# Four fused stages on one core: the first batch's state-space sum and the weight quantisation are done by other engines, in another order

## The chip, the cores and the metric

One core of a Trainium2 chip. Time is microseconds (us) of the device for one execution of the whole program; the median of three runs counts.

## What is computed

x is 4 batches of 512 rows by 512 columns (fp32), ctx is 4 batches of 512 by 256. Four stages follow one another, each with a residual:

```python
x = x + tanh(g_xattn[0]) * mamba(ctx, layernorm(x))          # hidden from ctx, gate from x
x = x + tanh(g_ffn[0])   * bit_ffn(layernorm(x))             # silu(gate) * val, then out; hidden 2048
x = x + tanh(g_xattn[1]) * cross_attention(layernorm(x), ctx) # 16 heads of 128, keys and values from ctx
x = x + tanh(g_ffn[1])   * experts(layernorm(x))             # 4 experts, row j goes to expert j % 4
# inside mamba, for each of 512 channels and 16 states n, over the 512 positions t:
state = state * exp(delta_t * A) + delta_t * u_t * B_t
y_t   = sum_n state_n * C_t,n  +  D * u_t ;  y = y * silu(z)
# inside bit_ffn every linear layer works on rounded numbers:
x_q = clip(round(x * 127 / max|x|), -128, 127) / scale ;  w_q = clip(round(w / mean|w|), -1, 1) * mean|w|
```

## The kernel before

One program holds six streams of work. M is mamba, F the bit feed-forward with the turn of x for the attention (XT), Q the quantisation of the three feed-forward weights, K the keys and values of all batches, A the attention (64 heads: 16 for each batch, then the output projection every 4 heads), E the experts. Each stream is a list of parts (`MAMBA`, `FFN`, `QUANT`, `KV`, `ATTN`, `EXP`), and each engine has a generator for each stream that issues its instructions of the next part. Which stream an engine serves next is fixed when the program is built: `plan()` places all parts on the engines by costs written in the code (for instance `("DVE", 2.45)` for a scan) and by priorities (`FIRST`), and each engine then issues in that order. So an engine never overtakes: where an instruction waits for a semaphore, all that stands behind it on that engine waits too.

What depends on what: M(0) must end before F(0) starts; F(b) before the attention of batch b; all of K (4 quarters of the heads by 4 batches, 16 groups) before the first head; M(b+1) and F(b+1) run beside the attention of batch b. TensorE (PE) fills its time with K as long as batch 0 is in M and F, and with A afterwards.

Mamba, per batch: convolution of 4 taps (`conv`, ScalarE L1171 copies, DVE L882 and L885), silu (L1175), two projections (`xp`, `dt`: L572, L1178, L581, L1183, L1184), softplus (`exp` L1187, `one` L889 and L1192, `soft` L898 to L906), then `init` (D * u, L911) and the loop over 16 states by 2 halves of the channels, so 32 terms of 128x1024. A term is `mul` (L922: delta*u times B), `scan` (L927), `out` (L932: times C), all on DVE, with both operands in SBUF. ScalarE makes the decays exp(delta*A) two instructions a term (L1164) into two buffers, one term ahead. The term is then added into `u` by a DMA that accumulates, issued by GpSimd:

```python
e.dma_start(u[:, 2 * g:2 * g + 2, :], two(wy[s]), accum_op=ALU.add).then_inc(S[f"d_w{s}"], 16)
```

Three buffers `wy` hold terms; `mul` of term i waits until term i-3 is added. B and C come broadcast from HBM (`s_bc<-bc_scratch`, L1524). After the loop: row statistics of x (`ln`, L824 to L828, and a power on GpSimd, L1367), `hn` (L943, waits for the last three additions), silu (L1202), `gate` (L947), four transposes on PE (`yt`, L589) and the residual (L950).

Quantisation, for the three weights w = 0 to 2 in four pieces c of 128x2048: load into a staging buffer (SP, L1471, L1473), sum of |w| on ScalarE (`abs`, L1146), the total through PE (L545), its inverse on DVE (L843 to L847), two DVE passes (L854: times the inverse, at most 1; L856: at least -1, plus MAGIC, which rounds) and a ScalarE pass to fp8 (`put`, L1151). `bias` does the bias rows (L861 to L869, ScalarE L1154). F(0) waits for all 12 `put`.

Feed-forward, for each tile t of 128 rows: entry `e` (statistics; L976, L978, `quant_row` L954 to L962; 5 transposes L611), 4 parts `m` of two banks (matmuls L600; tanh L1220; DVE L1003, L1011), leave `l`: maximum of |h| over 128x2048 (L1014), `quant_row` on 2048 columns (L960, L962), 16 transposes (L637), copies (L1226), 16 matmuls (L645), residual (L1026). K on PE: L679 (keys), L684 (values), L691 (norms), with ScalarE copies L1246, L1249, L1252. The attention starts with L710.

## Time and profile before

| what | us |
|---|---|
| three runs | 2015.21, 2017.95, 2027.63 (median 2017.95) |
| the profiled execution's own time | 2014.32 |
| its span, first to last instruction | 2012.5 |
| first scan of M(0) starts, last ends | 84.8, 253.0 |
| M(0) has written x | 284.6 |
| F(0) starts to normalise | 307.0 |
| first matmul of the attention | 472.2 |

The page gives busy time by engine. A busy share is an average over stages with different limits, so the stages are read one by one: the rows below give, for stretches of the span, the busy time of each engine and the granted clock of TensorE as a share of 2.4 GHz (0.5 is the level 1.2 GHz). The timeline gives start and duration of single instructions, with the idle time of the engine before them and what ended it.

### The profile page before, as it was taken

Reading aid. Unit: us, or ns where it says so; the run is one execution under the profiler, and the core shown is the slowest. Engines: PE = TensorE matmul, PEld = TensorE weight load, DVE = VectorE, ACT = ScalarE, POOL = GpSimd, SP = SyncE. Lnnn points to the kernel's source line nnn. Section 1 sums busy time; section 2 is a strip of 40 time slices with the busy share of each in tenths; the row PEclk is TensorE's granted clock in tenths of the full one; section 3 lists DMA queues with packets and bytes.
Section 4 is the critical chain, followed back from the end, with each engine's and each line's share of the span. In section 5 each row is a group of like instructions: output and inputs, shape, how many; then the busy total and the mean of one; then the engine's idle time right before and its main releaser. Section 6 shows DMA issues by size and latency. Waiting matters only on the chain.

```text
span 2012.5 us, 20103 instructions
## 1 busy us (share of the span) xinstructions
PE 1856.5 (92%) x6442; PEld 884.7 (44%) x6442; DVE 1386.6 (69%) x2076; ACT 936.6 (47%) x1848; POOL 616.6 (31%) x621
## 2 busy tenths in 40 slices
PE   7799998977998799999978999999998989999999
PEld 3355453433444234544433454444444434444543
DVE  4789876899996869988865999896764354431321
ACT  5856565544754355654624555654433333330100
POOL 1133321123644114454610335554312342320100
PEclk8789988988999889999988999999999999999999
DMA  6699952176775003887810257884101399874210
GB/s 236 210 265 284 275 181 101 53 202 154 195 194 140 12 22 94 206 207 186 205 56 18 58 152 180 243 199 117 43 21 59 112 277 272 254 208 183 94 52 32
DMA packets 159463, 304.40 MB, mean 151 GB/s; under 512 B 13944, under 2 KB 46968, under 8 KB 156416
## 3 DMA queue, kind: packets, MB, share of 16 engines
q1 hardware_dynamic: 140928, 236.01, 37.5%
q0 software_dynamic: 18432, 67.12, 17.2%
...
HBM read 177.64 MB, written 58.33 MB: 117 GB/s over the span
## 4 chain that ended last, share of the span: by engine, by line
PE 72%; DVE 11%; ACT 5%; issue 4%; DMA 4%; POOL 2%; SPq 1%; DVEq 0%; ACTq 0%; POOLq 0%
PE p L757 9%; PE p L710 8%; PE p L747 8%; PE p L727 8%; PE p L684 6%; PE p L794 6%; PE p L679 4%; PE p L600 4%; PE p L733 4%; PE p L691 3%; PE p L809 3%; PE p L645 2%; DMA s_U<-in_Wq 2%; PE p L581 1%; DVE s_U L1057 1%
## 5 line engine op out<-in xcount | busy, mean ns | idle before, releaser
L927 DVE TENSOR_TENSOR_SCAN s_M<-s_M 128x1024 f32<-128x1024 f32 x128 | 302.9, 2367 | 18.2 <-ACT s_M L1164 15.7
L1057 DVE CUSTOM_DVE_ANT_0 s_U<-p,s_U 128x512 f32<-128x512 f32 x256 | 187.3, 744 | 171.5 <-PE p L727 169.1
L727 PE MATMUL p<-s_U 128*128 128x512 f32 x512 | 269.3, 613 | 1.8 <-DMA s_U<-k_scratch 1.2
L710 PE MATMUL p<-s_U 128*128 128x512 f32 x512 | 254.7, 604 | 12.7 <-DMA s_U<-in_Wq 11.0
L1383 POOL DMA_DIRECT2D s_u<-s_M x128 | 113.5, 887 | 436.4 <-DVE s_M L932 395.7
L1427 POOL TENSOR_SCALAR s_U<-s_U 128x512 f32<-128x512 f32 x256 | 227.7, 913 | 5.9
L757 PE MATMUL p<-s_U 128*128 128x512 f32 x512 | 223.6, 592 | 0.0
L747 PE MATMUL p<-s_U 128*128 128x512 f32 x472 | 212.9, 594 | 2.4 <-DMA s_U<-p_scratch 1.6
L1294 ACT ACTIVATE s_U<-s_U 128x512 f32<-128x512 f32 x256 | 181.8, 719 | 57.4 <-DVE s_U L1061 57.4
L1299 ACT COPY s_U<-p 128x512 f32<-128x512 f32 x196 | 107.0, 591 | 173.8 <-PE p L733 170.3
L1164 ACT ACTIVATE s_M<-s_dl,s_small 128x511 f32<-128x511 f32 x256 | 170.3, 717 | 33.0 <-DVE s_M L927 32.8
L1423 POOL TENSOR_TENSOR s_U<-s_U,s_mone 128x4 f32<-128x4 f32 x64 | 79.5, 1242 | 294.6 <-ACT s_U L1294 294.4
L922 DVE TENSOR_TENSOR s_M<-s_du,s_bc 128x1024 f32<-128x1024 f32 x128 | 157.1, 1227 | 12.9 <-DMA s_bc<-bc_scratch 8.7
L932 DVE TENSOR_TENSOR s_M<-s_M,s_bc 128x1024 f32<-128x1024 f32 x128 | 156.3, 1221 | 2.3
L757 PEld LDWEIGHTS p<-s_U 128*128 128x128 f32 x512 | 96.8, 190 | 119.0 <-issue 118.6
L710 PEld LDWEIGHTS p<-s_U 128*128 128x128 f32 x512 | 95.0, 195 | 111.3 <-issue 95.2
L684 PE MATMUL p<-s_U 128*128 128x512 f32 x256 | 136.3, 675 | 5.9 <-ACT s_U L1249 2.6
L747 PEld LDWEIGHTS p<-s_U 128*128 128x128 f32 x472 | 89.6, 191 | 116.6 <-issue 114.1
L600 PE MATMUL p<-s_wq,s_U 128*128 128x512 fp8e4 x512 | 136.3, 414 | 0.0
L1367 POOL TENSOR_TENSOR s_U<-s_U,s_mhalf 128x4 f32<-128x4 f32 (+1 forms) x80 | 96.0, 1200 | 128.4 <-ACT s_U L1288 105.5
L679 PE MATMUL p<-s_U 128*128 128x512 f32 x256 | 116.1, 601 | 16.1 <-ACT s_U L1252 14.5
L727 PEld LDWEIGHTS p<-s_U 128*128 128x128 f32 x512 | 88.3, 193 | 81.8 <-issue 78.6
(178 smaller groups left out, 2509.4 us busy)
## 6 DMA issues: line engine op xcount, KB each, us to landing
s_u<-s_M POOLq DMA_DIRECT2D x128, 512.0 KB, 7.3
s_bc<-bc_scratch SPq DMA_DIRECT2D x128, 256.0 KB, 4.9
...
```

The lines of the kernel that those rows point to most:

```text
L600: ins = e.matmul(banks[bk][:], xT[t % 2][:, k, :], wt[:, k, ch * 512:(ch + 1) * 512], start=False, stop=(k == 3))
L679: ins = e.matmul(banks[bk][:], wk[:, k, i * 128:(i + 1) * 128], cT[b][:, k, :], start=(k == 0), stop=(k == 1))
L684: ins = e.matmul(banks[bk][:], cT[b][:, k, i * 128:(i + 1) * 128], wv[:, k, :], start=(k == 0), stop=(k == 1))
L710: ins = e.matmul(banks[bk][:], wqq[j % 2][:, k, :], axT[b % 2][:, k, :], start=(k == 0), stop=(k == 3))
L727: e.matmul(banks[bk][:], qT[j % 3][:, k * 128:(k + 1) * 128], kT[j % 2], start=True, stop=True).then_inc(S["a_s"], 1)
L747: ins = e.matmul(banks[bk][:], V[v][:, kt, :], now[:, kt], start=(kt == 0), stop=(kt == 3))
L757: ins = e.matmul(banks[bk][:], OT[h][:, k * 128:(k + 1) * 128], wo[h], start=(i == 0), stop=(i == GH - 1))
L927: e.tensor_tensor_scan(w, dA[i % 2], w, 0.0, ALU.mult, ALU.add).then_inc(S["m_s"], 1)
L1057: e.tensor_tensor_reduce(out=Pm[j % 2][:, k, :], in0=banks[ABANK[kind, j, k]][:], in1=rkb[j % 2], scale=rq[:, k:k + 1], scalar=-3.0e38, op ...
L1164: e.activation(av[:, t, 1:512], dl[:, 2 * g + t, 1:512], ACT.Exp, scale=Aneg[:, 2 * g + t, n:n + 1]).then_inc(S["m_da"], 1)
L1294: e.activation(Pm[j % 2][:, k, :], Pm[j % 2][:, k, :], ACT.Exp, bias=nm[:, k:k + 1], scale=1.0, accum_out=sm[:, k:k + 1]).then_inc(S["a_e" ...
L1427: e.tensor_scalar(P, P, rc[:, k - 1:k], 1.0, ALU.mult, ALU.mult).then_inc(S["a_pd"], 1)
```

## The change

It has four parts.

1. In batch 0, GpSimd adds each term into `u` itself (a tensor_tensor add of 128x1024, both operands in SBUF) in place of the accumulating DMA. Batches 1 to 3 keep the DMA. D * u moves behind the first scan, the zero columns of the decay buffers are set inside `soft`, and `init` (the first decays) moves between the two halves of `soft`.
2. Quantisation: `thr` (total and inverse), then for each piece `rnd` on ScalarE (scale, plus MAGIC, in place), `clip` on DVE (between MAGIC-1 and MAGIC+1), `put` on ScalarE. The staging loads of w = 1 and 2 are issued by ScalarE behind the `put` that frees the buffer.
3. The planner gets these parts with costs, later loads for the first pieces (17, 4, 9 and 5 in place of 5 each), and the priority on DVE is AFQMKE in place of AFMQKE. Its GpSimd cost for an addition is 2.6. So the order changes on every engine.
4. Feed-forward, all batches: the maximum of |h| is taken in four pieces, one behind each `m`, and a small one over the four; the last pass of `quant_row` on h is cut in two so that the first 8 transposes wait for half; the 5th transpose of the entry waits for its padding alone. Some semaphores are merged; the scores' matmul now waits for `a_qs` (the square behind the copy) in place of `a_qc`.

```diff
-    QUANT += [("abs", w, c) for c in range(4)] + [("put", w, c) for c in range(4)]
+    QUANT += [("abs", w, c) for c in range(4)] + [("thr", w, 0)]
+    for c in range(5):
+        QUANT += [("rnd", w, c)] if c < 4 else []
+        QUANT += [("put", w, c - 1)] if c else []
+        QUANT += [("clip", w, c)] if c < 4 else []
...
-MAMBA += [("soft", i) for i in range(8)] + [("init", 0)]
+MAMBA += [("soft", i) for i in range(4)] + [("init", 0)] + [("soft", i) for i in range(4, 8)]
...
-            part((kind, i), [("DVE", 1.3), ("POOL", 0.8), ("SUM", 5.0)])
+            part((kind, i), [("DVE", 1.3)] + ([("POOL", 0.8), ("SUM", 5.0)] if b else [("POOL", 2.6)]))
...
-FIRST = {"PE": "MFAQKE", "DVE": "AFMQKE", "ACT": "AFMQKE", "POOL": "MAFQKE", "DMA": "QMAFKE", "SUM": "MAFQKE"}
+FIRST = {"PE": "MFAQKE", "DVE": "AFQMKE", "ACT": "AFMQKE", "POOL": "MAFQKE", "DMA": "QMAFKE", "SUM": "MAFQKE"}
...
-                        e.tensor_scalar(src, src, thr[:, w:w + 1], 1.0, ALU.mult, ALU.min).then_inc(*v.up())
-                        e.wait_ge(*v.now())
-                        e.tensor_scalar(src, src, -1.0, MAGIC, ALU.max, ALU.add).then_inc(S["q_rnd"], 1)
+                    elif kind == "clip":
+                        e.wait_ge(S["q_rnd"], 4 * w + c + 1)
+                        e.tensor_scalar(stg[c], stg[c], MAGIC - 1.0, MAGIC + 1.0, ALU.max, ALU.min).then_inc(S["q_cut"], 1)
...
+                    elif kind == "rnd":
+                        e.activation(stg[c], stg[c], ACT.Copy, bias=MAGIC, scale=thr[:, w:w + 1]).then_inc(S["q_rnd"], 1)
...
+                        if w < 2:
+                            e.wait_ge(S["q_put"], i + 1)
+                            load_stage(e, w + 1, c)
...
-                        e.dma_start(u[:, 2 * g:2 * g + 2, :], two(wy[s]), accum_op=ALU.add).then_inc(S[f"d_w{s}"], 16)
+                            e.wait_ge(*added(b, i - 2))
+                        y = u[:, 2 * g:2 * g + 2, :]
+                        if b:
+                            e.dma_start(y, two(wy[s]), accum_op=ALU.add).then_inc(S[f"d_w{s}"], 16)
+                        else:
+                            e.tensor_tensor(y, y, two(wy[s]), ALU.add).then_inc(S["m_ad"], 1)
...
-                        e.wait_ge(S["f_hq"], 4 * b + t + 1)
+                        e.wait_ge(S["f_hq"], 2 * (4 * b + t) + k)
...
+                        e.tensor_reduce(qt[:, 24 + ch:25 + ch], h[:, ch * 512:(ch + 1) * 512], AXX, ALU.max, apply_absolute_value=True).then_inc(*v.up())
...
-                        e.tensor_reduce(qt[:, 16:17], h, AXX, ALU.max, apply_absolute_value=True).then_inc(*v.up())
+                        e.tensor_reduce(qt[:, 16:17], qt[:, 24:28], AXX, ALU.max).then_inc(*v.up())
```

How the order moves, at three places. First GpSimd, from its first norm of K on: `s_krs` are the norms of K, `s_u` the sum of mamba, `s_M` a term. Before:

```order
L1367 TENSOR_TENSOR s_krs<-s_krs,s_mhalf 128x16
L1383 DMA s_u<-s_M 128x1024
L1367 TENSOR_TENSOR s_krs<-s_krs,s_mhalf 128x16
L1383 DMA s_u<-s_M 128x1024 x3
L1367 TENSOR_TENSOR s_krs<-s_krs,s_mhalf 128x16
```

And now:

```order
L1397 TENSOR_TENSOR s_krs<-s_krs,s_mhalf 128x16
L1416 TENSOR_TENSOR s_u<-s_u,s_M 128x1024 x2
L1397 TENSOR_TENSOR s_krs<-s_krs,s_mhalf 128x16
L1416 TENSOR_TENSOR s_u<-s_u,s_M 128x1024 x6
L1397 TENSOR_TENSOR s_krs<-s_krs,s_mhalf 128x16
```

The 32 DMA issues of batch 0 have become 32 adds, with the norms of K strewn between them: fewer norms for as many terms than before.

Second DVE, from the last passes of `soft` to the second scan (L927 before, L941 now, where `s_M` is written from `s_M` alone; in the row before it both name `s_du`). `s_wab`, `s_gam`, `s_thr` and 128x2048 are quantisation. Before:

```order
L906 TENSOR_TENSOR s_du<-s_dl,s_u 128x1024
L843 TENSOR_REDUCE s_wab<-s_wab 128x1
L845 TENSOR_SCALAR s_gam<-p 128x1
L847 RECIPROCAL s_thr<-s_gam 128x1
L852 TENSOR_SCALAR s_U<-s_U,s_thr 128x512
L854 TENSOR_SCALAR s_U<-s_U,s_thr 128x2048
L856 TENSOR_SCALAR s_U<-s_U 128x2048
L911 TENSOR_SCALAR s_u<-s_u,s_small 128x512 x4
L913 MEMSET s_M 128x2 x2
L922 TENSOR_TENSOR s_M<-s_du,s_bc 128x1024
L854 TENSOR_SCALAR s_U<-s_U,s_thr 128x2048
L856 TENSOR_SCALAR s_U<-s_U 128x2048
```

And now:

```order
L923 TENSOR_TENSOR s_dl<-s_dl,s_M 128x1024
L877 TENSOR_SCALAR s_U<-s_U 128x2048
L925 TENSOR_TENSOR s_dl<-s_dl,s_du 128x1024
L877 TENSOR_SCALAR s_U<-s_U 128x2048
L927 TENSOR_TENSOR s_du<-s_dl,s_u 128x1024
L929 MEMSET s_M 128x2
L936 TENSOR_TENSOR s_M<-s_du,s_bc 128x1024
L877 TENSOR_SCALAR s_x<-s_x 128x2048
L941 SCALAR_TENSOR_TENSOR s_M<-s_M 128x1024
L945 TENSOR_SCALAR s_u<-s_u,s_small 128x512 x4
L877 TENSOR_SCALAR s_U<-s_U 128x2048
L950 TENSOR_TENSOR s_M<-s_M,s_bc 128x1024
```

In the old order weight 0 is quantised ahead of these rows and weight 1 at them; now it is weight 0 here, with three `clip` ahead of the first scan and one behind it. The eight `clip` of weights 1 and 2 and the five bias passes stand among later terms of M(0); before, the last two pieces of weight 1, the bias and weight 2 stood behind its last term.

Third PE, around the transposes of M(0) (L589 before, L610 now). Before:

```order
L679 MATMUL p<-s_U 128x512 x8
L684 MATMUL p<-s_U 128x512 x2
L589 MATMUL p<-s_identf,s_M 128x128 x8
L684 MATMUL p<-s_U 128x512 x2
L691 MATMUL p<-s_ones,s_U 128x1 x16
L589 MATMUL p<-s_identf,s_M 128x128 x8
```

And now:

```order
L702 MATMUL p<-s_U 128x512 x8
L707 MATMUL p<-s_U 128x512 x4
L610 MATMUL p<-s_identf,s_M 128x128 x8
L714 MATMUL p<-s_ones,s_U 128x1 x16
L610 MATMUL p<-s_identf,s_M 128x128 x8
L707 MATMUL p<-s_U 128x512 x2
```

The neighbourhood is alike, the place is not: before, 96 of the 128 key matmuls stand ahead of the first transpose, so 12 of the 16 groups of K; now 80, so 10. On ScalarE the four `abs` of weight 0, which stood among the convolution's copies and around silu, now stand behind silu (two of them) and around `exp`.

## Rows read from the trace of the kernel before

**Rows 1.** The page: span, and busy time by engine.
```profile
span 2012.5 us, 20103 instructions
PE 1856.5 (92%) x6442; PEld 884.7 (44%) x6442; DVE 1386.6 (69%) x2076; ACT 936.6 (47%) x1848; POOL 616.6 (31%) x621
```

**Rows 2.** Windows by stage: us; PE, PEld, DVE, ACT, POOL busy; clock, DMA share, GB/s.
```profile
73.00:254.00 181.00, 178.81 (x620) 98.45 (x619) 156.60 (x109) 108.11 (x196) 63.40 (x40) 0.93 0.99 272
...
285.00:307.00 22.00, 19.92 (x46) 8.70 (x45) 16.61 (x22) 15.14 (x21) 4.58 (x3) 0.95 0.24 85
307.00:472.00 165.00, 141.31 (x578) 69.34 (x576) 132.45 (x205) 73.99 (x124) 30.05 (x24) 0.86 0.43 124
...
654.00:804.00 150.00, 130.59 (x520) 55.53 (x519) 122.05 (x230) 67.52 (x122) 35.88 (x34) 0.89 0.18 43
```

**Rows 3.** DVE by line, 84 to 254 us: busy us, mean ns, idle before, releasers.
```profile
L927 DVE TENSOR_TENSOR_SCAN s_M<-s_M 128x1024 f32<-128x1024 f32 x32 | 73.3, 2292 | 15.2 <-ACT s_M L1164 14.5
L932 DVE TENSOR_TENSOR s_M<-s_M,s_bc 128x1024 f32<-128x1024 f32 x32 | 39.2, 1225 | 1.1
L922 DVE TENSOR_TENSOR s_M<-s_du,s_bc 128x1024 f32<-128x1024 f32 x31 | 37.8, 1220 | 4.7 <-DMA s_u<-s_M 3.9 <-DMA s_bc<-bc_scratch 0.5
L856 DVE TENSOR_SCALAR s_U<-s_U 128x2048 f32<-128x2048 f32 x1 | 1.2, 1226 | 0.0
```

**Rows 4.** Timeline of POOL and DVE where they meet: start us, us, instruction.
```profile
763.17 0.70 POOL L1427 TENSOR_SCALAR s_U<-s_U 128x512 f32<-128x512 f32 x1
...
763.28 1.66 DVE L922 TENSOR_TENSOR s_M<-s_du,s_bc 128x1024 f32<-128x1024 f32 x1
...
763.85 1.66 POOL L1427 TENSOR_SCALAR s_U<-s_U 128x512 f32<-128x512 f32 x1
...
591.35 2.61 DVE L927 TENSOR_TENSOR_SCAN s_M<-s_M 128x1024 f32<-128x1024 f32 x1
...
591.80 2.66 POOL L1427 TENSOR_SCALAR s_U<-s_U 128x512 f32<-128x512 f32 x1
```

**Rows 5.** POOL by line, whole span.
```profile
L1383 POOL DMA_DIRECT2D s_u<-s_M x128 | 113.5, 887 | 436.4 <-DVE s_M L932 395.7 <-DMA s_u<-s_M 31.1 <-issue 9.7
...
L1399 POOL TENSOR_TENSOR s_x<-s_x,s_obt 128x512 f32<-128x512 f32 x16 | 20.3, 1268 | 62.9 <-DVE s_U L976 62.9
```

**Rows 6.** Timeline of ACT and DVE up to the first scan.
```profile
29.10 1.91 ACT L1146 ACTIVATE s_U<-s_x 128x2048 bf16<-128x2048 f32 x1 [4.15 <-DMA s_x<-in_gateT]
...
62.23 1.23 DVE L898 SCALAR_TENSOR_TENSOR s_M<-s_M 128x1024 f32<-128x1024 f32 x1 [3.28 <-ACT s_dl L1192]
...
76.25 0.16 DVE L845 TENSOR_SCALAR s_gam<-p 128x1 f32<-128x1 f32 x1 [3.89 <-PE p L545]
...
84.76 2.29 DVE L927 TENSOR_TENSOR_SCAN s_M<-s_M 128x1024 f32<-128x1024 f32 x1
```

**Rows 7.** Timeline of DVE from the last term of M(0) to F(0).
```profile
253.00 1.22 DVE L932 TENSOR_TENSOR s_M<-s_M,s_bc 128x1024 f32<-128x1024 f32 x1
...
258.17 1.28 DVE L854 TENSOR_SCALAR s_x<-s_x,s_thr 128x2048 f32<-128x2048 f32 x1
...
283.00 1.60 DVE L950 SCALAR_TENSOR_TENSOR s_x<-p,s_gts,s_x 128x512 f32<-128x512 f32 x2 [5.21 <-PE p L589]
...
307.04 0.55 DVE L976 TENSOR_SCALAR s_U<-s_x,s_fq 128x512 f32<-128x512 f32 x1 [0.74 <-POOL s_fq L1367]
```

**Rows 8.** The chain: norms of two successive groups of K, and the attention's start.
```profile
159.21 3.47 PE p L691 x32
...
176.52 3.46 PE p L691 x32
...
472.19 3.69 PE p L710 x8
```

**Rows 9.** DVE by line, whole span: leaving a tile of the feed-forward.
```profile
L1014 DVE TENSOR_REDUCE s_fq<-s_U 128x1 f32<-128x2048 f32 x16 | 36.5, 2278 | 0.2
...
L962 DVE TENSOR_SCALAR s_U<-s_U 128x2048 bf16<-128x2048 f32 x16 | 20.4, 1274 | 0.6
```

More of the change, by code:

```diff
@@ L229, in forward @@
             if k % 2:
-                part(name, [("DVE", 1.6)], ("m", t, k - 1), free=pair)
+                part(name, [("DVE", 2.3)], ("m", t, k - 1), free=pair)
             else:
@@ L242, in forward @@
         elif k == 0:
-            part(name, [("DVE", 5.4)], ("m", t, 7))
+            part(name, [("DVE", 3.6)], ("m", t, 7))
         elif k < 3:
@@ L540, in pe_quant @@
                 for kind, w, c in QUANT:
-                    if kind == "put" and c == 0:
+                    if kind == "thr":
                         e.wait_ge(S["p_set"], 8)
@@ L839, in dve_quant @@
                 for kind, w, c in QUANT:
-                    if kind == "put":
-                        if c == 0:
+                    if kind == "thr":
                             e.wait_ge(S["q_abs"], 4 * w + 4)
@@ L927, in dve_mamba @@
                         e.tensor_tensor_scan(w, dA[i % 2], w, 0.0, ALU.mult, ALU.add).then_inc(S["m_s"], 1)
+                        if i == 0:
+                            e.wait_ge(S["m_h0"], 2 * b + 2)
+                            for t in range(4):
+                                e.tensor_scalar(u[:, t, :], u[:, t, :], Dv[:, t:t + 1], None, ALU.mult).then_inc(*v.up())
                     elif kind == "out":
                         n, g = divmod(i, 2)
-                        w = two(wy[term(b, i)[0]])
+                        w = two(wy[term(b, i)])
                         e.wait_ge(S["m_s"], 32 * b + i + 1)
@@ L951, in dve_mamba, with quant_row @@
                     yield
-            def quant_row(src, amax, dst, sc, mul, last):
+            def quant_row(src, amax, dst, sc, mul, done):
                 e.tensor_scalar(sc[:, 0:1], amax, mul, EPS, ALU.mult, ALU.max).then_inc(*v.up())
@@ L961, in quant_row @@
                 e.wait_ge(*v.now())
-                e.tensor_scalar(dst, src, MAGIC, 127.0, ALU.subtract, ALU.min).then_inc(*(last or v.up()))
+                n = src.shape[1] // len(done)
+                for i, up in enumerate(done):
+                    e.tensor_scalar(dst[:, n * i:n * i + n], src[:, n * i:n * i + n], MAGIC, 127.0, ALU.subtract, ALU.min).then_inc(*up)
             def dve_ffn(b):
@@ L1508, in sp_quant @@
                 for kind, w, c in QUANT:
-                    if kind == "abs" and (w or c >= 2):
-                        load_stage(w, c)
+                    if kind == "abs" and w == 0 and c >= 2:
+                        load_stage(e, w, c)
                     if (kind, w, c) == QUANT[-1]:
```

117 lines of the change are left out of this document (59 added, 58 removed).

## The prediction

> **What bounds the kernel now.** I read the page first: TensorE is busy 92% of the span [rows 1], so time can only come from its idle time, its clock, or the order of the start. Then the windows by stage [rows 2]. From 73 to 254 us PE is busy 178.8 of 181 us, all with K, while DVE runs M(0)'s loop. From 307 to 472 PE is busy 141.3 of 165 us: 23.7 us idle, at a mean clock of 0.86. A feed-forward stretch beside attention (654 to 804) has 19.4 us idle; the two later ones have 18 and 9. In the attention between them PE is nearly full. So the chain is M(0), F(0), the attention's start at 472.2 us [rows 8], and from there 1540 us in which PE sets the pace. What delays the attention's start is paid at the end nearly in full, because PE can do no A before it and has only K to fill with.
>
> M(0)'s loop is DVE's [rows 3]: 73.3 + 39.2 + 37.8 = 150.3 us of scans and products between 84.8 and 254.2 us, thus 4.7 us a term, and about 19 us idle, 14.5 of it waiting for ScalarE's decays. The accumulating DMAs cost DVE only 3.9 us there. So the DMA that is replaced is hardly on the path.
>
> **GpSimd's adds, the term that decides.** The trace has no GpSimd instruction of 128x1024, but it shows what one does to DVE [rows 4]. Alone, L1427 takes 0.70 us. At 763.17 it starts; DVE's product L922 starts at 763.28 and takes 1.66 us where it takes 1.22 [rows 3]: it stood until L1427 ended at 763.87. The next L1427, started at 763.85, took 1.66 us: it stood until the product had read, and ended 0.56 us behind it. A scan fares alike: 2.61 us in place of 2.29 with L1427 ahead of it, and the L1427 behind took 2.66. They take turns, and neither runs beside the other. All three DVE instructions of a term are of this kind, each with both inputs in SBUF. In the old batch 0 GpSimd only issued DMAs there, 0.89 us each [rows 5], and the products kept their 1.22 us.
>
> The Trainium skill ("SBUF — State Buffer", section "Who interferes with whom") says that a DVE instruction with two SBUF inputs and a GpSimd instruction that reads SBUF exclude each other for the whole instruction, also when DVE is in no fast mode. The rows agree with it, for GpSimd instructions with one input; by the rule the whole add would be exclusive as well, which gives the sum below, and a hold shorter than the add gives the second rival.
>
> The add's own length: 128x512 with two inputs takes 1.268 us [rows 5]. For 128x1024 I take 2.4 us (twice that less some fixed part; bounds 1.27 and 2.54). The same skill ("GPSIMD Engine Reference", section 3.1 "Elementwise — side-by-side cycle accounting") lists 4497 ns for 2048 elements, so an estimate of 2.25 us by that page; the sum would be 5 us lower.
>
> Cost on DVE: 32 x 2.4 = 77 us. Bounds: 0 if the adds fall beside DVE, 32 x 2.54 = 81 us.
>
> **Up to the first scan.** Before, ScalarE's copies and silu stand behind `abs`, one of which waited 4.15 us for its load until 29.1 [rows 6]. Now silu can start at about 24 in place of 31.1, and of the four quantisation passes of 1.91 us between silu and Ln two remain in the way: L898 starts at about 52 in place of 62.2. From there to the first scan were 22.5 us; now I take 20: 9.8 for `soft`, 3.7 for three clips, 1.2 for the product, 1 for the inverse, 4 for PE's total as at 76.25 [rows 6]. First scan at 72: 13 us early (bounds 5 and 18, by how far ScalarE's rounding passes hold up the clips).
>
> **The loop.** The same 150.3 us; nine clips of 1.23 [rows 3] make 11.1; five bias passes, four of them like a 1.22 us product, 5.4; D * u and two inverses 3.1: together 170. Two waits for PE's total, 4 each: 8. The 77 us of adds. The old wait for decays goes: ScalarE gets 77 us more time, which also covers most of its 24 rounding and writing passes. Sum 255; the last term ends at 72 + 255 = 327, where it was 254.2 [rows 7]: 73 us late.
>
> **From there to F(0).** Before: 30.4 us until x was written at 284.6, with four passes of two pieces (5 us), the bias and 5.2 us for PE's transposes in between [rows 7]; then 22.4 us until 307.04, which were weight 2. Now all this lies in the loop. I take 22 us (statistics 4, `hn` 1.9, silu and gate 4, transposes with a norm group between them 10, residual 2) and 2.5 us. F(0) starts at 327 + 24.5 = 351.5: 44.5 us late.
>
> **F(0) beside the rest of K.** Before the transposes of M(0), PE has 10 groups of K in its queue and not 12. A group is 17.3 us (176.52 - 159.21 [rows 8]); ten of them are done long before 345, so PE stands still for some 100 us and may not go on, and the two groups, 34.6 us, come behind it. Of the 23.7 us idle there [rows 2] I let half be filled by them, and the finer waits give 3: 34.6 - 12 - 3 = +20 us. The attention starts at 472 + 44.5 + 20 = 536.5.
>
> **The finer waits.** Per tile the maximum of 2.28 us becomes a small one of 0.15 behind a piece of about 0.7, and half of the 1.27 us pass comes off the first transposes [rows 9]: 1.4 + 0.6 = 2.0 us a tile from the chain. For the 12 tiles of batches 1 to 3 that is 24 us at most, and attention covers part of it: I take 10 (bounds 0 and 24). DVE has 0.6 us more per tile. The scores' wait for the square costs nothing, since the square stands a head earlier.
>
> **Sum.** 2014.3 + 44.5 + 20 - 10 = 2069 us, against the profiled execution's own time of 2014.3. The median of the runs is 3.6 us above that, which is less than I can resolve; I leave it out.
>
> **Rivals.**
> First, the same, but nothing is won back: K's two groups come in full (+34.6), the finer waits give nothing, and M(0) is 10 us later still because clips wait for ScalarE. 2014.3 + 44.5 + 34.6 + 10 = 2103. For it: every engine issues in a fixed order that was planned without the blocking. Against it: idle time of 23.7 us is there to fill.
> Second, half a price: the add holds DVE up only for about 1.27 us. The loop loses 36 us less: 2069 - 36 = 2033. For it: no row has an add beside a product. Against it: L1427 blocks for its whole length.
> Third, the adds lie beside DVE. Then the loop is 178 us, but ScalarE's extra passes (24 of 1.91 us beside decays and K's copies, at 108 of 181 us busy [rows 2]) keep the 15 us wait for decays: 193, last term at 265, F(0) at 289.5, 17.5 us early; K's groups +20, waits -10: 2007. Rows 4 speak against it.
> Fourth, on the other side: nothing blocks, the decays come in time too, K fills all 23.7 us, and the finer waits give all they can. F(0) at 274.5 (-32.5), +34.6 - 23.7 - 8 = +3, -24: 2014 - 53 = 1961. Its mechanism is F(0) starting early, because the quantisation no longer stands between M(0) and F(0); it decides from the point where the scans keep 2.29 us beside the adds. For it: those 22 us are really there [rows 2, 7]. Against it: the loop is DVE's, and rows 4.
>
> **Chances.** The forecast 0.48 (its own range 2048 to 2090), first rival 0.17, second 0.14, third 0.13, fourth 0.08. A measurement of this kernel tells about 1% from no change, so 2038 and more is slower. The second case lies across that bound. Slower: 0.48 + 0.17 + 0.10 = 0.75; within 1%: 0.04 + 0.13 = 0.17; faster: 0.08. The range: below 2022 lie the last two cases without their upper tail, above 2102 part of the first, together about 0.2. So 2022 to 2102.
>
> **What the new profile would show.** GpSimd's adds of 2.4 us or more in the records (their wait counted in), scans and products of batch 0 with means well above 2.29 and 1.22 us, unlike those of batches 1 to 3; terms 7.2 us or more apart; the first scan near 72 and F(0) near 350; PE idle by some 100 us ahead of the transposes, with a lower granted clock there; the attention's start near 536. I am wrong if the scans of batch 0 stay at 2.29 us; if the terms lie under 6 us apart; or if PE goes on with K all through M(0).

## The result, and the profile after

The changed kernel takes 2071.02 us (median of 4 runs, 2064.48 to 2075.08), the kernel before 2016.68 (4 runs): a ratio of 1.0254, 95% interval 1.0205 to 1.0303, thus slower, by some 50 us. The prediction was 2069. The profiled execution of the changed kernel has a span of 2073.2 us, 60.7 more than the 2012.5 of the one before; it is the longest of its four and the one before a short one, so stages compared by these two show some 6 to 10 us more than the medians and the ratio do.

The page of the changed kernel:

```profile
span 2073.2 us, 20183 instructions
...
PE 1869.4 (90%) x6442; PEld 883.7 (43%) x6442; DVE 1438.7 (69%) x2144; ACT 959.2 (46%) x1860; POOL 695.5 (34%) x621
...
PE   8546889999699689998977999989999989999999
...
PEclk8767988899799889999988999999999999999999
...
L1416 POOL TENSOR_TENSOR s_u<-s_u,s_M 128x1024 f32<-128x1024 f32 x32 | 109.1, 3409 | 122.0 <-DVE s_M L950 122.0
...
```

PE is busy 90% of the span where it was 92% [rows 1]. The low digits of PE and of its clock stand in the first six slices, the first 310 us: the time was lost at the start. The windows by stage say how much (columns as in [rows 2]):

```profile
76.00:305.00 229.00, 154.22 (x462) 79.88 (x463) 223.86 (x121) 139.09 (x197) 139.58 (x38) 0.78 0.44 141
...
327.00:526.00 199.00, 190.22 (x742) 94.74 (x741) 159.96 (x247) 98.71 (x171) 45.87 (x31) 0.91 0.47 130
...
0.00:526.00 526.00, 424.35 (x1433) 214.49 (x1434) 425.30 (x434) 295.50 (x445) 198.90 (x90) 0.84 0.47 145
526.00:2073.00 1547.00, 1445.08 (x5009) 669.23 (x5009) 1013.40 (x1711) 663.74 (x1415) 496.62 (x532) 0.97 0.50 137
...
```

The last two lines split the span at the first matmul of the attention. Up to there PE stands still for 526.0 - 424.4 = 101.7 us; before it were 472.2 - 412.4 = 59.8 us. So the attention starts 53.8 us late, of which 41.9 us are idle time. The other 12.0 us are PE busy for longer with the same work, and they go with a lower granted clock (0.78 in M(0)'s loop, where PE stops and starts; 0.93 in that stage before [rows 2]). Behind the attention's start the two differ by 1547.0 - 1539.8 = 7 us. M(0)'s loop alone holds 74.8 us of PE's idle time, where it held 2.2 [rows 2].

The milestones that the prediction spoke of, from the timeline of DVE and PE:

```profile
...
76.22 2.28 DVE L941 TENSOR_TENSOR_SCAN s_M<-s_M 128x1024 f32<-128x1024 f32 x1
...
304.77 1.23 DVE L950 TENSOR_TENSOR s_M<-s_M,s_bc 128x1024 f32<-128x1024 f32 x1
...
326.49 0.55 DVE L995 TENSOR_SCALAR s_U<-s_x,s_fq 128x512 f32<-128x512 f32 x1 [0.73 <-POOL s_fq L1397]
...
526.01 2.04 PE L733 MATMUL p<-s_U 128*128 128x512 f32 x2 [4.46 <-DMA s_U<-in_Wq]
```

First scan at 76.2 (84.8 [rows 6]), last term done at 306.0 (254.2 [rows 7]), F(0) normalises at 326.5 (307.0 [rows 7]), attention at 526.0 (472.2 [rows 8]). So F(0) starts 19.5 us late, and from F(0) to the attention another 34 us are lost, though PE is idle there for 8.8 us only (327 to 526), 4.5 of them for the load of Wq in the last row. It does K that was left over. By line, PE's products with the keys' weights (16 to a group of K) in that stretch, before (307 to 472) and now (two fences):

```profile
L679 PE MATMUL p<-s_U 128*128 128x512 f32 x48 | 22.0, 594 | 1.6 <-ACT s_krs L1257 1.6
```

```profile
L702 PE MATMUL p<-s_U 128*128 128x512 f32 x96 | 44.0, 601 | 0.3 <-ACT s_krs L1287 0.3
```

So six groups were left at F(0)'s start, and before only three.

DVE in M(0)'s loop, by form; and, in the second fence, one term in the timeline of DVE and GpSimd, with the last add behind it:

```profile
L941 DVE TENSOR_TENSOR_SCAN s_M<-s_M 128x1024 f32<-128x1024 f32 x32 | 112.3, 3508 | 2.5 <-ACT s_M L1195 1.6
L950 DVE TENSOR_TENSOR s_M<-s_M,s_bc 128x1024 f32<-128x1024 f32 x32 | 50.9, 1591 | 0.8
...
L877 DVE TENSOR_SCALAR s_U<-s_U 128x2048 f32<-128x2048 f32 x7 | 10.6, 1514 | 0.0
...
```

```profile
231.87 1.22 DVE L936 TENSOR_TENSOR s_M<-s_du,s_bc 128x1024 f32<-128x1024 f32 x1
233.12 4.32 DVE L941 TENSOR_TENSOR_SCAN s_M<-s_M 128x1024 f32<-128x1024 f32 x1
...
237.47 1.22 DVE L950 TENSOR_TENSOR s_M<-s_M,s_bc 128x1024 f32<-128x1024 f32 x1
238.61 1.22 DVE L936 TENSOR_TENSOR s_M<-s_du,s_bc 128x1024 f32<-128x1024 f32 x1
239.86 2.29 DVE L941 TENSOR_TENSOR_SCAN s_M<-s_M 128x1024 f32<-128x1024 f32 x1
...
232.03 3.26 POOL L1416 TENSOR_TENSOR s_u<-s_u,s_M 128x1024 f32<-128x1024 f32 x1 [3.48 <-DVE s_M L950]
235.25 4.89 POOL L1397 TENSOR_TENSOR s_krs<-s_krs,s_mhalf 128x16 f32<-128x16 f32 x1
...
306.07 2.35 POOL L1416 TENSOR_TENSOR s_u<-s_u,s_M 128x1024 f32<-128x1024 f32 x1 [3.48 <-DVE s_M L950]
...
310.61 3.20 POOL L1397 TENSOR_TENSOR s_krs<-s_krs,s_mhalf 128x16 f32<-128x16 f32 x1
...
305.91 0.69 DVE L847 BATCH_NORM_STATS2 s_st<-s_x 128x6 f32<-128x512 f32 x1
...
310.04 1.91 DVE L960 TENSOR_SCALAR s_M<-s_x,s_st 128x512 f32<-128x512 f32 x4
...
```

The scan is read with the GpSimd row beside it. The add is issued at 232.03, behind the end of `out`. DVE's `mul` has started at 231.87 and keeps its 1.22 us; the add stands until it is over, at 233.09, and runs then. The scan, issued at 233.12, takes 4.32 us in place of 2.29 [rows 3]: it stood for 2.03 us. The scan at 239.86 has no add in front and takes 2.29; the add's place there is taken by the power on 128x16, issued at 235.25, which takes 4.89 us between DVE's instructions, 3.20 at 310.61, where DVE first runs passes of one input (L960), and 2.93 in e1 below, where DVE is idle beside it. It does not hold DVE as the adds do: while it runs, DVE's `out`, `mul` and scan keep 1.22, 1.22 and 2.29 us. A term is 6.74 us (238.61 - 231.87) and was 4.7. The last add has no DVE instruction with two SBUF inputs beside it: it takes 2.35 us, and DVE's statistics beside it keep their 0.69. Summed over the loop, against the means before [rows 3]: scans +39, `out` +12, `mul` +4, the clips L877 +2, and +2 on one bias pass (L885, 3.19 us here, 1.28 in e1 below): 59 us.

What PE waited for before F(0) (columns: us in total, times, longest), and the timeline of PE and ScalarE in the longest of these stops:

```profile
PE p L702 <- ACT s_krs L1287: 45.1, 4, 20.2
...
```

```profile
...
137.03 3.78 PE L702 MATMUL p<-s_U 128*128 128x512 f32 x4 [20.17 <-ACT s_krs L1287]
...
106.40 0.57 ACT L1282 COPY s_U<-p 128x512 f32<-128x512 f32 x1
111.75 3.90 ACT L1172 ACTIVATE s_U<-s_U,s_thr 128x2048 f32<-128x2048 f32 x2 [4.78 <-DVE s_thr L869]
...
116.77 1.90 ACT L1177 ACTIVATE s_wq<-s_U 128x2048 fp8e4<-128x2048 f32 x1
...
119.14 2.00 ACT L1172 ACTIVATE s_x<-s_x,s_thr 128x2048 f32<-128x2048 f32 x1 [0.47 <-ACT s_wq L1177]
...
133.01 1.91 ACT L1177 ACTIVATE s_wq<-s_U 128x2048 fp8e4<-128x2048 f32 x1 [2.80 <-DVE s_U L877]
...
136.32 0.58 ACT L1282 COPY s_U<-p 128x512 f32<-128x512 f32 x1
136.79 0.19 ACT L1287 ACTIVATE s_krs<-p 128x16 f32<-128x16 f32 x1
...
```

PE does not stand for want of K. It has K in its queue, and waits for K's banks: from 116.9 to 137.0 for L1287, the norms' copy. ScalarE took a K copy at 106.40 and the next at 136.32; in between stand the four rounding passes of weight 1 (L1172, two of them in one row), its four writing passes (L1177), three pairs of decays and a bias cast (not all shown), with a wait of 4.8 us for the inverse of weight 1's total (L869) and one of 2.8 us for a clip (L877). ScalarE issues in its fixed order, so the copies that would free PE's banks wait behind the quantisation.

### The profile page after: what moved, and what is told of

Same layout as the page of the kernel before. It is cut to its first block, busy times and chain, and to the rows that moved or that the text cites. A ratio compares the mean times of both kernels' runs of the same rounds, so it can differ in the third digit from the quotient of the medians.

```text
span 2073.2 us, 20183 instructions
## 1 busy us (share of the span) xinstructions
PE 1869.4 (90%) x6442; PEld 883.7 (43%) x6442; DVE 1438.7 (69%) x2144; ACT 959.2 (46%) x1860; POOL 695.5 (34%) x621
## 4 chain that ended last, share of the span: by engine, by line
PE 62%; DVE 12%; issue 8%; ACT 6%; DMA 5%; POOL 5%; SPq 1%; ACTq 0%; DVEq 0%; POOLq 0%
PE p L780 7%; PE p L733 7%; PE p L770 7%; PE p L750 7%; PE p L621 5%; PE p L817 5%; DVE s_M L941 5%; PE p L702 4%; PE p L707 3%; PE p L832 3%; PE p L756 3%; PE p L668 2%; DMA s_u<-s_M 2%; POOL s_U L1460 2%; DMA s_U<-in_Wq 2%
## 5 line engine op out<-in xcount | busy, mean ns | idle before, releaser
L941 DVE TENSOR_TENSOR_SCAN s_M<-s_M 128x1024 f32<-128x1024 f32 x128 | 341.6, 2669 | 15.8 <-ACT s_M L1195 12.9
L750 PE MATMUL p<-s_U 128*128 128x512 f32 x512 | 271.7, 619 | 12.7 <-DMA s_U<-k_scratch 8.3
L733 PE MATMUL p<-s_U 128*128 128x512 f32 x512 | 257.8, 611 | 14.9 <-DMA s_U<-in_Wq 14.6
L780 PE MATMUL p<-s_U 128*128 128x512 f32 x512 | 223.8, 593 | 0.0
L770 PE MATMUL p<-s_U 128*128 128x512 f32 x472 | 212.6, 593 | 3.2 <-ACT s_U L1329 2.1
L1460 POOL TENSOR_SCALAR s_U<-s_U 128x512 f32<-128x512 f32 x256 | 210.6, 853 | 5.8
L1414 POOL DMA_DIRECT2D s_u<-s_M x96 | 86.1, 899 | 344.1 <-DVE s_M L950 336.7
L702 PE MATMUL p<-s_U 128*128 128x512 f32 x256 | 125.2, 639 | 56.4 <-ACT s_krs L1287 45.3
L1456 POOL TENSOR_TENSOR s_U<-s_U,s_mone 128x4 f32<-128x4 f32 x64 | 88.5, 1383 | 259.9 <-ACT s_U L1324 259.9
L707 PE MATMUL p<-s_U 128*128 128x512 f32 x256 | 147.3, 719 | 25.9 <-ACT s_U L1279 11.6
L950 DVE TENSOR_TENSOR s_M<-s_M,s_bc 128x1024 f32<-128x1024 f32 x128 | 168.4, 1316 | 2.3
L1416 POOL TENSOR_TENSOR s_u<-s_u,s_M 128x1024 f32<-128x1024 f32 x32 | 109.1, 3409 | 122.0 <-DVE s_M L950 122.0
L780 PEld LDWEIGHTS p<-s_U 128*128 128x128 f32 x512 | 96.8, 190 | 119.0 <-issue 118.1
L733 PEld LDWEIGHTS p<-s_U 128*128 128x128 f32 x512 | 95.8, 196 | 118.6 <-issue 102.8
L1397 POOL TENSOR_TENSOR s_U<-s_U,s_mhalf 128x4 f32<-128x4 f32 (+1 forms) x80 | 101.4, 1267 | 132.2 <-ACT s_U L1318 116.6
L770 PEld LDWEIGHTS p<-s_U 128*128 128x128 f32 x472 | 89.2, 190 | 115.3 <-issue 111.0
```

Source lines behind the costliest of these rows:

```text
L702: ins = e.matmul(banks[bk][:], wk[:, k, i * 128:(i + 1) * 128], cT[b][:, k, :], start=(k == 0), stop=(k == 1))
L707: ins = e.matmul(banks[bk][:], cT[b][:, k, i * 128:(i + 1) * 128], wv[:, k, :], start=(k == 0), stop=(k == 1))
L733: ins = e.matmul(banks[bk][:], wqq[j % 2][:, k, :], axT[b % 2][:, k, :], start=(k == 0), stop=(k == 3))
L750: e.matmul(banks[bk][:], qT[j % 3][:, k * 128:(k + 1) * 128], kT[j % 2], start=True, stop=True).then_inc(S["a_s"], 1)
L770: ins = e.matmul(banks[bk][:], V[v][:, kt, :], now[:, kt], start=(kt == 0), stop=(kt == 3))
L780: ins = e.matmul(banks[bk][:], OT[h][:, k * 128:(k + 1) * 128], wo[h], start=(i == 0), stop=(i == GH - 1))
```

## The experiments

Twelve kernels, in four groups, each group beside executions of the kernel before on the same chip. The kernel before had medians of 2024.1, 2025.3, 2027.1 and 2024.0 us in the four groups, so kernels are compared by ratio (with its 95% interval), and spans of different groups only roughly. The times in the table are those of each profiled execution; "idle" is PE's idle time up to the attention's start.

| run | last scan ends | F(0) | attention | idle | span | ratio to before |
|---|---|---|---|---|---|---|
| before | 253.0 | 307.0 | 472.2 | 59.8 | 2012.5 | 1 |
| changed | 304.7 | 326.5 | 526.0 | 101.7 | 2073.2 | 1.0254 |
| e1 changed, adds by DMA | 271.3 | 293.5 | 493.3 | 72.8 | 2042.8 | 1.0127 |
| e2 the same, replanned | 271.4 | 303.5 | 504.0 | 75.1 | 2054.5 | 1.0132 |
| e3 before + adds | 297.3 | 351.0 | 516.3 | 86.2 | 2063.3 | 1.0190 |
| e4 before + finer waits | 261.1 | 314.2 | 479.2 | 59.8 | 2021.5 | 0.9991 |
| e5 changed, half adds | 276.8 | 297.0 | 497.5 | 75.6 | 2044.0 | one time |
| e6 changed, K first | 304.6 | 321.7 | 488.3 | 58.8 | 2042.5 | 1.0094 |
| e7 e2 + K first | 289.1 | 313.2 | 476.7 | 56.0 | 2034.0 | 1.0063 |
| e8 changed, priced plan | 340.1 | 368.5 | 525.6 | 94.0 | 2084.1 | 1.0316 |
| e9 e7, rounding on DVE | 287.3 | 312.7 | 470.0 | 60.6 | 2029.4 | 1.0044 |
| e10 e2, rounding on DVE | 299.0 | 325.8 | 488.3 | 52.7 | 2044.9 | 1.0075 |
| e11 before + late loads | 251.6 | 304.2 | 466.2 | 48.5 | 2034.2 | 1.0049 |
| e12 e7, twelve groups | 265.0 | 288.2 | 448.2 | 39.4 | 2012.8 | 0.9969 |

**e1: the adds undone, order kept.**

```diff
...
-                        if b:
-                            e.dma_start(y, two(wy[s]), accum_op=ALU.add).then_inc(S[f"d_w{s}"], 16)
-                        else:
-                            e.tensor_tensor(y, y, two(wy[s]), ALU.add).then_inc(S["m_ad"], 1)
+                        e.dma_start(y, two(wy[s]), accum_op=ALU.add).then_inc(S[f"d_w{s}"], 16)
```

> The changed kernel, with the 32 terms of the first batch added by accumulating DMAs again, and every engine's order left as it is in the changed kernel. Lock theory (each GpSimd add keeps DVE from reading for about 2.03 us, the length that its scans gained): scans of batch 0 back to 2.29 us, terms about 4.8 us apart, the last term ends near 240 (305 in the changed kernel), the attention starts near 461 (526), total 2071 - 65 = 2006 us, 1998 to 2016. Rival (the order is what costs: fewer K groups ahead, extra quantisation passes in the loop): the loop gets shorter but PE gains little, total above 2040. Rival (DVE's price, but DMA adds now stand behind the weight loads): terms over 5.5 us apart, total near 2030.

Measured: 2051.75 us, ratio 1.0127 (1.0083 to 1.0170). Scans are back at 2.29 us, and this half of the theory holds. The total does not: by the ratios 26 us came back, not 65. DVE by form, PE's waits, and the windows:

```profile
L941 DVE TENSOR_TENSOR_SCAN s_M<-s_M 128x1024 f32<-128x1024 f32 x32 | 73.3, 2290 | 22.6 <-ACT s_M L1195 22.1
...
```

```profile
PE p L702 <- ACT s_krs L1287: 37.8, 4, 16.8
...
```

```profile
...
73.00:240.00 167.00, 117.46 (x337) 61.18 (x338) 138.21 (x103) 119.66 (x161) 44.03 (x32) 0.74 0.86 236
...
```

Now the scans wait 22.1 us for decays (1.6 us in the changed kernel), and the loop ends at 271 and not at 240. Still PE has 49.5 us idle between 73 and 240, with the same wait for L1287. The remaining 1.3% is therefore the rest of the change, of which the next runs take the parts.

**e2: the planner's cost back as well** (`[("POOL", 0.8), ("SUM", 5.0)]` for each `out`).

> As the run before, and the planner's cost of a term also back to that of a DMA. K's groups ahead of M(0)'s transposes stay ten, so I expect the same as the run before within 6 us: 2000 to 2012 us. If the order planned with a GpSimd add of 2.6 us were part of the loss, it would be over 10 us faster than the run before.

Measured: 2051.36 us, ratio 1.0132 (1.0087 to 1.0178). As e1: how the planner priced the adds is no part of the loss. The level that I expected missed for e1's reason.

**e3: the adds alone, on the kernel before.**

```diff
...
+                        if b:
                             e.dma_start(y, two(wy[s]), accum_op=ALU.add).then_inc(S[f"d_w{s}"], 16)
+                        else:
+                            e.tensor_tensor(y, y, two(wy[s]), ALU.add).then_inc(S["m_ad"], 1)
```

> The kernel before with the adds of the first batch on GpSimd alone, its order left as it was (one semaphore is shared to make room). Lock theory: 32 x 2.03 = 65 us on DVE, of which the old wait for decays, about 15 us, is given back: the last term ends near 254 + 50 = 304, the attention starts near 472 + 50, total 2013 + 50 = 2063 us, 2052 to 2078. Rival (adds lie beside DVE, the order costs): scans stay at 2.29 us and the total within 10 us of the kernel before.

Measured: 2062.73 us, ratio 1.0190 (1.0145 to 1.0234), 38 us. The last scan ends 44 us late, F(0) and the attention start 44 us late.

```profile
L929 DVE TENSOR_TENSOR_SCAN s_M<-s_M 128x1024 f32<-128x1024 f32 x32 | 115.9, 3623 | 3.9 <-ACT s_M L1165 2.8
L934 DVE TENSOR_TENSOR s_M<-s_M,s_bc 128x1024 f32<-128x1024 f32 x32 | 56.9, 1778 | 1.1
...
```

As the lock theory has it: +60 us of DVE (42.6 on scans, 17.7 on `out`), less some 16 us of waits: 11.7 for decays and 3.9 for DMA adds, which are gone. So the adds alone do delay M(0)'s end by what their hold costs, on the old order. The total of 2063 that was expected came out by luck: it was +50 us on 2013, and the kernel before took 2024 here, so +38 was measured. A later start is not paid in full at the end.

**e4: the finer waits alone, on the kernel before.**

```diff
...
+                        e.wait_ge(S["f_h"], i + 1)
+                        e.tensor_reduce(qt[:, 24 + ch:25 + ch], h[:, ch * 512:(ch + 1) * 512], AXX, ALU.max, apply_absolute_value=True).then_inc(*v.up())
...
-                        quant_row(h, qt[:, 16:17], hq, qt[:, 18:20], 0.5, (S["f_hq"], 1))
+                        quant_row(h, qt[:, 16:17], hq, qt[:, 18:20], 0.5, [(S["f_hq"], 1)] * 2)
```

> The kernel before with the finer waits of the feed-forward alone (a maximum per piece of 512, the last pass in two halves, the fifth transpose's own wait), with their planner costs. The prediction's term was -10 us (0 to -24): 2003 to 2009 us. The changed kernel's windows suggest that what the feed-forwards gain (12 us of PE's idle time) is lost again in the attention between them: then 2012 to 2018 us, no difference.

Measured: 2021.95 us, ratio 0.9991 (0.9963 to 1.0019): no difference. The merged semaphores and the scores' later wait are not in this run; none holds them apart. The waits of PE in a feed-forward beside attention, in the kernel before and in the changed one (two fences):

```profile
PE p L611 <- DVE s_U L989: 10.1, 3, 4.9
...
PE p L637 <- DVE s_U L962: 0.8, 1, 0.8
...
```

```profile
PE p L634 <- DVE s_U L981: 9.7, 3, 5.2
...
PE p L660 <- DVE s_U L981: 0.2, 1, 0.2
```

The wait that the change shortens, of the `ht` transposes, held PE for 0.8 us in the whole of F(1). What holds it is the entry of a tile: 10.1 us before, released by the last copy of 1/scale (L989); 9.7 us now, released by the pass ahead of those copies (L981), and the fifth transpose then waits another 0.9 us for them. In F(0) one such wait is long, 11.0 us in the kernel before, and the finer waits left 9.6 of it (e4).

**e5: half of each add.** `y[:, 0:1, :]` and the first half of the term in place of the whole.

> The changed kernel with GpSimd adding only the first half of each term (128x512 of 128x1024): the other half of every term of the first batch is left out. If the add's hold on DVE goes with its size, it falls from 2.03 to about 1.0 us: scans of batch 0 that start behind an add take 3.3 us in place of 4.3, terms 5.7 us apart in place of 6.72, the last term ends near 273. If the hold is a fixed cost of a turn, terms stay above 6.4 us apart. Total: 2041 us if the end moves one to one with the last term, about 2052 us (as with DMA adds) if K's backlog holds the attention's start.

Measured: 2045.8 us, one time. Timeline of DVE and GpSimd:

```profile
231.11 1.23 DVE L950 TENSOR_TENSOR s_M<-s_M,s_bc 128x1024 f32<-128x1024 f32 x1
...
233.51 3.24 DVE L941 TENSOR_TENSOR_SCAN s_M<-s_M 128x1024 f32<-128x1024 f32 x1
236.78 1.23 DVE L950 TENSOR_TENSOR s_M<-s_M,s_bc 128x1024 f32<-128x1024 f32 x1
...
278.12 1.27 POOL L1416 TENSOR_TENSOR s_u<-s_u,s_M 128x512 f32<-128x512 f32 x1 [3.49 <-DVE s_M L950]
...
```

A scan behind a half add takes 3.24 us, so it stood 0.95 us, and a term is 5.67 us (236.78 - 231.11). The hold goes with the size. Alone the half add takes 1.27 us, the whole one 2.35; the holds are 0.95 and 2.03, so the hold is about 0.32 us shorter than the instruction's record at either size. The last scan ends 28 us earlier than in the changed kernel (said: 32), and F(0) starts 29.5 us earlier (e1: 33). The total, one time only, is 1.010 of its group's median of the kernel before, near e1's 1.0127: taking away half of each add gave back about as much as taking away all of it.

**e6: K ahead of the quantisation on ScalarE, adds kept.**

```diff
-FIRST = {"PE": "MFAQKE", "DVE": "AFQMKE", "ACT": "AFMQKE", "POOL": "MAFQKE", "DMA": "QMAFKE", "SUM": "MAFQKE"}
+FIRST = {"PE": "MFAQKE", "DVE": "AFQMKE", "ACT": "AFMKQE", "POOL": "MAFQKE", "DMA": "QMAFKE", "SUM": "MAFQKE"}
```

> The changed kernel, its GpSimd adds kept, with one thing changed in the planner: ScalarE takes K's copies and squares ahead of the quantisation passes, not behind them. Backlog theory (the 75 us that PE stands still in M(0)'s loop are PE waiting for ScalarE's K copies, which stand in a fixed order behind rounding and writing passes, and all the K left undone comes behind F(0)): 13 K groups ahead of the transposes in place of ten, PE idle in the loop 30 us or less, F(0) to the attention's start about 160 us in place of 199, attention starts near 492, total about 2040 us (2030 to 2050). Rival (PE's idle time in the loop is of no account, or the decays now come late and the scans wait): the total stays within 8 us of the changed kernel's 2071.

Measured: 2043.42 us, ratio 1.0094 (1.0062 to 1.0126), 32 us less than the changed kernel by the ratios.

```profile
...
69.00:305.00 236.00, 215.85 (x683) 115.41 (x681) 226.32 (x127) 170.69 (x249) 147.42 (x42) 0.86 0.55 177
...
322.00:488.00 166.00, 137.56 (x534) 65.52 (x532) 129.57 (x228) 68.08 (x112) 26.98 (x21) 0.83 0.36 99
...
```

```profile
PE p L702 <- ACT s_krs L1287: 10.9, 2, 6.4
...
```

The loop is as long as before, ending at 304.6, and PE is idle in it for 20 us in place of 75; the wait for L1287 fell from 45.1 to 10.9 us. F(0) starts 4.8 us and the attention 37.7 us earlier. This is the second cause, shown by a change of two letters in the planner's priorities; with them K's groups ahead of the transposes go from ten to 13 1/4, so the run shows the order as a whole and not the one wait alone.

**e7: both.** e2 with e6's line.

> Both: terms of the first batch added by accumulating DMAs, and K ahead of the quantisation on ScalarE. By both theories together PE's idle time before the attention falls from 72 us (adds by DMA, quantisation first) to about 35: the attention starts near 458, total about 2013 us (2005 to 2022), at most equal to the kernel before. If only the lock mattered it would equal the run with DMA adds in the old order, 2051 us.

Measured: 2036.5 us, ratio 1.0063 (1.0029 to 1.0098). The attention starts at 476.7, not at 458. Without adds the scans should be early; they stood 32.1 us for decays, and ScalarE stood 64.0 us for K's products of PE, with the decays queued behind:

```profile
ACT s_U L1282 <- PE p L707: 40.4, 22, 13.0
ACT s_U L1276 <- PE p L702: 23.6, 24, 5.9
...
DVE s_M L941 <- ACT s_M L1195: 32.1, 15, 8.0
...
```

So the 2013 us expected were missed by 23. With 13 1/4 (e6) and 13 1/2 K groups (here) ahead of M(0)'s transposes the kernel with adds and the one without end within 0.3% of each other, less than their intervals resolve; that K's products and copies hold up both is what the waits suggest. Whether the number of groups or ScalarE's extra passes do it was left for e9 and e12.

**e8: the planner told what an add costs** (2.05 us more of DVE for each scan of batch 0), adds kept.

> The changed kernel, its GpSimd adds kept, with the planner told that each scan of the first batch takes DVE 2.05 us more. It then puts 14 K groups ahead of M(0)'s transposes in place of ten, the quantisation still first on ScalarE. Backlog theory: about 30 us won back, total near 2041 us (2030 to 2052). If an order can't help because the engines run out of time in the loop, the total stays above 2063.

Measured: 2087.94 us, ratio 1.0316 (1.0279 to 1.0353), the slowest: the backlog theory's 2041 was a miss, and the second reading (above 2063) came out. With 14 groups ahead of the transposes ScalarE stood 100.4 us for PE and the scans 44.0 us for decays; terms are late, and M(0) ends at 340. K then ran out on PE in the middle of F(0), which holds 39 us of idle time. As the waits read, it is not engine time as such: the plan puts K's copies on ScalarE earlier than PE delivers them, and the decays wait behind.

**e9 and e10: who rounds.** e7 and e2, with the rounding again two passes of DVE:

```diff
...
+                    elif kind == "rnd":
+                        e.tensor_scalar(stg[c], stg[c], thr[:, w:w + 1], 1.0, ALU.mult, ALU.min).then_inc(S["q_rnd"], 1)
...
-                        e.tensor_scalar(stg[c], stg[c], MAGIC - 1.0, MAGIC + 1.0, ALU.max, ALU.min).then_inc(S["q_cut"], 1)
+                        e.tensor_scalar(stg[c], stg[c], -1.0, MAGIC, ALU.max, ALU.add).then_inc(S["q_cut"], 1)
```

> The run with DMA adds and K ahead of the quantisation, with the rounding back on DVE in two passes as in the kernel before: ScalarE has 12 passes of about 1.95 us (23 us) less, DVE 12 of about 1.2 us (15 us) more. If ScalarE's fixed order is what still makes the scans late there (22 to 32 us of waits for decays), the last term ends near 275 in place of 289 and the total falls to about 2022 us. If PE is already the bound up to the attention (207 of 224 us busy in the loop), it stays at the ratio of that run, 1.006 of the kernel before, within 6 us.

> The replanned run with DMA adds, quantisation first on ScalarE, with the rounding back on DVE in two passes. It holds ScalarE's 12 rounding passes apart from the move of the quantisation into the loop. If those 23 us ahead of K's copies are what PE waits for there (51 us idle in the loop), the idle time falls by 20 us or more (K groups ahead of the transposes go from ten to 13), the total from 1.0132 to about 1.005 of the kernel before. If it is the place of the quantisation and not who does it, the ratio stays above 1.01.

Measured: e9 2032.39 us, ratio 1.0044 (1.0020 to 1.0068), the last scan ends at 287.3 where e7's does at 289.1. By this ScalarE's 23 us are not what keeps e7's loop long, though with 14 1/2 K groups ahead of the transposes, one more than in e7, the two are not wholly held apart. e10 2041.75 us, ratio 1.0075 (1.0037 to 1.0114), PE's idle time between the first scan and the transposes 15.7 us, where e2 has 51.5. So moving the rounding off ScalarE is worth about 0.6% of e2's 1.3%, between my two readings, with intervals that still overlap; e7, with K first and the rounding on ScalarE, gains 0.7% on e2. The 0.75% that is left in e10 no run takes apart; its first scan comes 8 us later than e2's.

**e11: the loads' times alone, on the kernel before.**

```diff
-            out.append(("Q", [("DMA", 5.0), ("ACT", 2.0)], [(0, "put", w - 1, c)] if w else [], (0, kind, w, c), [], []))
+            out.append(("Q", [("DMA", 5.0 if w else (17.0, 4.0, 9.0, 5.0)[c]), ("ACT", 2.0)], [(0, "put", w - 1, c)] if w else [], (0, kind, w, c), [], []))
```

> The kernel before with one thing of the change: the planner is told that the first four weight loads land at 17, 4, 9 and 5 us and no longer 5 each. Silu then stands ahead of three of the maxima and of weight 0's passes. PE's idle time before the first scan (28.4 us) falls by about 10, the first scan comes at about 75 (84.8), K's count ahead of the transposes stays at 12. Total 8 us less than the kernel before: ratio about 0.996 (0.992 to 1.000). If what is gained early is lost again because weight 0's passes then stand in the loop, the ratio is 1.000 or above.

Measured: 2035.35 us, ratio 1.0049 (1.0025 to 1.0073), slower. The start behaved: idle time ahead of the first scan 13.4 us (28.4), first scan at 74.6, attention at 466.2, 6 us early. From there to the end it took 1568 us, where before took 1540 in another group; by the ratio some 16 us were lost there. An early attention is not all: the order behind it was planned anew as well, and what was gained early was lost there more than once over.

**e12: e7 with fewer K groups in front.**

```diff
-        does = {"k": [("PE", 1.75), ("ACT", 1.2)], "v": [("PE", 1.75), ("ACT", 0.6)], "n": [("PE", 3.7)], "nv": [("ACT", 0.25), ("POOL", 3.0)],
+        does = {"k": [("PE", 2.05), ("ACT", 1.2)], "v": [("PE", 2.05), ("ACT", 0.6)], "n": [("PE", 3.7)], "nv": [("ACT", 0.25), ("POOL", 3.0)],
```

> The run with DMA adds and K ahead of the quantisation, with the planner's PE time of a K product set from 1.75 to 2.05 us, so that it puts 12 K groups ahead of M(0)'s transposes as in the kernel before, in place of 13 1/4. In that run ScalarE waited for PE's K products with decays queued behind (DVE stood 32 us for decays) and PE had no K left at the end of F(0) (29 us idle). If the number of groups is what decides between these two, the last term ends near 272 (289 there), the idle time between F(0) and the attention falls by 10 us, and the ratio comes to 0.998 of the kernel before (0.994 to 1.003). If it is the 24 more passes of ScalarE that keep the decays late, the last term stays above 283 and the ratio at 1.006.

Measured: 2018.9 us (12 runs), ratio 0.9969 (0.9949 to 0.9988): faster than the kernel before by 0.3%, and the only version here whose interval lies below 1. It keeps the rounding on ScalarE, so the first of the two readings holds: the number of groups decides between e7 and this.

```profile
...
DVE s_M L941 <- ACT s_M L1195: 6.9, 4, 3.8
...
```

```profile
0.00:448.20 448.20, 408.77 (x1439) 209.10 (x1439) 341.56 (x418) 288.54 (x438) 112.30 (x85) 0.90 0.69 202
448.20:2012.00 1563.80, 1452.80 (x5004) 674.18 (x5004) 1041.55 (x1727) 672.89 (x1425) 508.90 (x536) 0.96 0.51 137
...
```

Decays cost 6.9 us in place of e7's 32.1, the last scan ends at 265.0, and PE is idle 39.4 us before the attention, which starts 24 us earlier than in the kernel before. Behind it the run takes 1564.6 us against 1540.3, so most of it is given back: all 24 us by these two spans, some 18 by the ratio.

## Why the prediction was right, and where it was not

The total came out, 2071 against 2069, as a sum of three errors that nearly cancel, and that is luck. In the profiled executions, for which the sum was made: F(0) +19.5 (said +44.5), from F(0) to the attention +34.3 (said +20), behind it +6.9 (said -10): 2014.3 + 60.7 = 2075. What was right is the mechanism that decides, and its sign.

**The adds as a lock: right in kind, 18 us too dear.** Scans and products of batch 0 are longer beside adds, by half as much beside half adds (e5) and not at all without (e1). So the third and fourth rivals are out, and the second, with 1.27 us for the whole add, too. The add's own length was taken as 2.4 us and is 2.35. The wrong term is 32 x 2.4 = 77 us: a scan stands 2.03 us and not the record's length, 32 x 2.03 = 65, of which 59 were paid in the loop. The Trainium skill ("SBUF — State Buffer", section "Who interferes with whom") has the one that comes second stand for the whole of the other's instruction; for the adds the trace agrees but for 0.32 us by which the hold is shorter than the add's record, and for the power on 128x16 it does not, since `out` and `mul` kept their 1.22 us beside it. That section also has DVE's fast modes blocked, with one input as well: the clip L877, whose median is 1.22 us for 2048 elements, as long as a product takes for 1024, took 3.38 us once in the loop, behind an add issued 1 us before it, which agrees. "Terms 7.2 us or more apart" was wrong with the price: they are 6.74 where no other pass stands between them. Over the whole loop, its other passes included, they are 229.8 / 32 = 7.2 apart, where the forecast's own 255 / 32 makes 8.0.

**First scan and loop.** First scan 76.2 where 72 was said. In the loop DVE's waits for PE's total were put at 8 us, and its idle time of all kinds is 229.0 - 223.9 = 5 us; its work without the adds' price is 223.9 - 59 = 165, said 170; the scans' wait for decays went, as said. Together: last term at 306.0, said 327, of which 18 us are the adds' price. To F(0) 20.5 us, said 24.5. So F(0) is 19.5 us late, not 44.5.

**K's backlog: 14 us too cheap, and for the wrong reason.** I took 34.6 us for two groups and let 12 be won back, 3 more by the finer waits. F(0) to the attention took 199.5 us where it took 165.2, 34.3 more, as in the first rival, but not by its way. The 12 were about right: PE's idle time there fell by 14.9 us (23.7 to 8.8). The groups were miscounted: two is the difference at the transposes, and before, PE did one more group between them and F(0), where the changed kernel has no time for one (19.9 of 22 us busy from 285 to 307 [rows 2]). At F(0)'s start three more groups were left, and PE was busy there for 190.2 us in place of 141.3, 48.9 more. The reasoning before it, that PE is through with ten groups long before the transposes and then stands still for some 100 us, is not what happened either. PE stood 74.8 us, in pieces of up to 20 us, and worked on K until the transposes at 316.6. The other step that failed is "ScalarE gets 77 us more time, which also covers most of its 24 rounding and writing passes". For the decays that was so. But these passes stand ahead of K's copies, and e6, which turns that priority round, wins back 32 of the 51 us. I had named as a sign of being wrong that "PE goes on with K all through M(0)": by that mark the picture of PE's queue was wrong, though the lower clock there (0.78) was as said.

**The finer waits: nothing, said 10.** e4 gives 0.9991. The 2.0 us a tile were worked out for DVE's chain, and PE's waits for that chain were never looked up: in F(1) they held 0.8 us (e4). In F(0) they held 11.0, of which the finer waits alone take 1.4 (e4), and in the changed kernel K fills them.

**How the causes add.** The adds cost 1.9% on the old order (e3), 1.3% on the new (changed against e1) and 0.3% with K first (e6 against e7), and the order 1.3% without adds (e1). 1.9 and 1.3 make 3.2 where 2.5 was measured, which the intervals do not separate; that the adds cost only 0.3% with K first is clearly less than 1.9. Both delay the same two things, M(0)'s end and K, which would explain it; no run shows it alone.

What stays open is why the stretch behind the attention's start grows when that start comes early (1540 us before, 1547 changed, 1565 in e12, 1568 in e11). In e12 PE's idle time there is 111.8 us against 96.2, in many small waits. The other 9 of its 24 us are PE busy for longer, at a clock of 0.96 against 0.97; executions of the kernel before differ as much (their mean clock is 0.935 to 0.946). No run took it apart.
